# Two key chunks per step in the second layer, 12,000-byte key rows, and another order of the work on TensorE

## The reference, cut to what matters

```python
x = x + tanh(g_xattn[i]) * xattn(layernorm(x), ctx, ctx, ...)
x = x + tanh(g_ffn[i]) * ffn(layernorm(x), ...)

# layer 0, differential attention: 32 heads of 4 dims for q and k
a1 = softmax(q1 @ k1.T * SCALE) @ v ; a2 = softmax(q2 @ k2.T * SCALE) @ v
attn = a1 - lam * a2                       # then rms norm, subln_w, output projection

# layer 1, masked attention: 16 heads of 8 dims
scores = where(mask, finfo.min, (x @ Wq.T + bq) @ (ctx @ Wk.T + bk).T / sqrt(8))
out = softmax(scores) @ (ctx @ Wv.T + bv)  # then output projection
```

## Time and profile before

| | |
|---|---|
| median of 3 runs | 2350.72 us (2350.26 to 2360.24) |
| the profiled execution | 2361.65 us, its span on the core 2359.2 us |
| mean granted TensorE clock | 0.946 of full speed |
| main loop of layer 0 | from about 117 us to 1225 us |
| main loop of layer 1 | from about 1455 us to 2179 us |
| busy shares of the span | PE 93%, DVE 71%, ACT 64%, POOL 54% |

### The profile page before, as it was taken

One profiled execution on the slowest core, in us unless ns is written; L12 is line 12 of the kernel. 1 busy time (PEld: TensorE's weight loads), 2 busy tenths in 40 slices (PEclk: granted clock), 3 DMA queues, 4 the chain that ended last, 5 costly groups with the idle time before them and its releaser, 6 DMA issues. The chain is left out here.

```text
span 2359.2 us, 67435 instructions
## 1 busy us (share of the span) xinstructions
PE 2192.7 (93%) x27256; PEld 1303.0 (55%) x27256; DVE 1677.1 (71%) x3697; ACT 1507.8 (64%) x2133; POOL 1278.9 (54%) x1418
## 2 busy tenths in 40 slices
PE   4799999999999999999967957999999999999798
PEld 3255555555555555555536843666655666666576
DVE  3688888888888888888816555777766677774644
ACT  2177788777877778778763322767666667766322
POOL 5335655655654554655333445777766777762232
PEclk8599999999999999999997975999999999999699
DMA  3635344344444444444201027667665666661100
GB/s 105 128 77 113 96 98 109 101 94 108 106 97 99 112 96 95 115 93 94 48 7 57 24 61 149 137 142 137 143 131 120 127 144 140 138 126 24 54 1 16
DMA packets 113421, 227.82 MB, mean 97 GB/s; under 512 B 46052, under 2 KB 58596, under 8 KB 112612
## 3 DMA queue, kind: packets, MB, share of 16 engines
q1 hardware_dynamic: 113124, 223.67, 42.8%
HBM read 146.77 MB, written 76.48 MB: 95 GB/s over the span
## 5 line engine op out<-in xcount | busy, mean ns | idle before, releaser
L1061 ACT ACTIVATE probs<-score_ps 125x896 f32<-125x896 f32 x1152 | 1014.3, 915 | 210.3 <-PE score_ps L954 207.9
L1119 DVE TENSOR_REDUCE max_part<-max_ps 112x1 f32<-112x500 f32 x1024 | 654.7, 668 | 115.3 <-PE spare_ps L923 68.3
L970 PE MATMUL acc_ps<-probs,vext 125*32 125x224 f32 (+1 forms) x12288 | 673.2, 316 | 6.6 <-issue 6.1
L923 PE MATMUL max_ps<-kstack,qstack 48*112 48x500 f16 x1535 | 508.1, 405 | 4.9 <-DVE max_part L1119 2.6
L954 PE MATMUL score_ps<-qstack,kstack 50*125 50x224 f16 (+1 forms) x6144 | 454.8, 244 | 17.2 <-ACT probs L1061 13.9
L954 PEld LDWEIGHTS score_ps<-qstack,kstack 50*125 50x125 f16 x6144 | 344.4, 134 | 183.8 <-issue 122.2
L1116 DVE CUSTOM_DVE_ANT_0 kstack<-max_ps,kstack 112x500 f32<-112x500 f32 x511 | 335.3, 675 | 134.2 <-PE max_ps L923 80.1
L1119 DVE TENSOR_REDUCE max_part<-spare_ps 112x1 f32<-112x500 f32 x512 | 343.3, 670 | 64.6 <-PE max_ps L923 63.5
L970 PEld LDWEIGHTS acc_ps<-probs,vext 125*32 125x32 f32 x12288 | 261.7, 109 | 225.8 <-issue 156.5
L923 PE MATMUL spare_ps<-kstack,qstack 48*112 48x500 f16 x769 | 310.7, 404 | 20.2 <-issue 16.9
L923 PEld LDWEIGHTS max_ps<-kstack,qstack 48*112 48x112 f16 x1535 | 173.5, 129 | 143.4 <-issue 77.7
(11 more groups left out here) (200 smaller groups left out, 2697.8 us busy)
## 6 DMA issues: line engine op xcount, KB each, us to landing
kstack<-k_parts SPq DMA_DIRECT2D x384, 187.5 KB, 6.6
k_parts<-khl SPq DMA_DIRECT2D x128, 375.0 KB, 2.8
ctx_f<-in_ctx SPq DMA_DIRECT2D x32, 750.0 KB
ctx_f<-context_parts SPq DMA_DIRECT2D x32, 750.0 KB, 4.4
context_parts<-ctx_f SPq DMA_DIRECT2D x16, 750.0 KB, 3.8
context_parts<-kstack SPq DMA_DIRECT2D x16, 750.0 KB, 3.5
mask_in<-in_mask SPq DMA_DIRECT2D x128, 82.0 KB
qrows<-q_parts SPq DMA_DIRECT2D x384, 7.0 KB, 7.0
```

Source lines behind the costliest of these rows:

```text
L923: nc.tensor.matmul(room(("P", n, p))[0:PIECE, 0:TK], qstack[n % SLOTS][rows, c, PIECE * i:PIECE * (i + 1)], kstack[n % SLOTS][rows, c, TK ...
L970: last = nc.tensor.matmul(acc_ps[32 * j:32 * j + 32, TT * S * i:TT * S * (i + 1)].rearrange("p (s c) -> p s c", s=S), vext[n % SLOTS][:, t ...
L1061: nc.scalar.activation(probs[t % 2][:, 896 * h:896 * h + 896].rearrange("k (b c) -> k b c", b=2), score_ps[(t * H + h) % 2][0:KT, :, 0:448 ...
L1119: nc.vector.reduce_max(best, scores, AX.X).then_inc(s_red, 1)
```

## The change

1. **Layer 1 steps over two chunks.** `steps` is 6 instead of 12 there. A step has two scores (one per chunk), two pairs of search pieces, one `weigh` that covers both chunks (16 matmuls), and its preparations are merged into steps 1 to 5 (`where`): F and V0, then V1 and V2, then M and K0, then K1 and K2, then A. They go into the two banks of the score half that the first exponential has read, no longer into the search rooms. F is one job of four transposes and one drain in place of two. `AHEAD` is 3 steps (12 pieces) instead of 5 (10 pieces).
2. **The order of a step.** `weigh` is one call everywhere. `order_of` chooses one of four written orders by whether this step and the one before have a preparation other than A or M. Layer 0: `scores 0, pair 0, weigh, scores 1, pair 1, prepare`, except t = 1, where both scores stand first. Layer 1: steps 0 and 1 have both scores first; steps 2 to 4 run `scores 0, weigh, scores 1, pair 0, prepare, pair 1`; step 5 runs `scores 0, pair 0, scores 1, weigh, pair 1, prepare`.
3. **Key rows.** The columns of Wk are permuted at setup (`key_order`), so that the four `PAIRS` rows of a partition lie side by side in DRAM. A fill DMA reads 16 rows of 12,000 bytes instead of 64 of 3,000. The layer-1 key bias is loaded once more in that order, by eight DMAs of ScalarE's queue.
4. **Queues in layer 1.** POOL makes the additive mask before the score mask; SP loads the next mask only after both are made, and issues the next context load after `fill_m`.

```diff
+        self.uses_f = self.halves
+        self.steps = NKT if self.halves == 2 else NKT // 2
...
+        key_bias = [(columns[HALF * r + c:HALF * (r + 1):PAIRS, 2:4],
+                     a["columns"][HALF * r + HALF // PAIRS * c:HALF * r + HALF // PAIRS * (c + 1), :]) for r in range(2) for c in range(PAIRS)]
...
-                        link(nc.vector.tensor_copy(high, weight))
-                        link(nc.vector.tensor_tensor(low, weight, high, ALU.subtract))
+                        for part in [(weight, high, low)] if w else key_order(i, weight, high, low):
+                            link(nc.vector.tensor_copy(part[1], part[0]))
+                            link(nc.vector.tensor_tensor(part[2], part[0], part[1], ALU.subtract))
...
-        where = {("V", 0): (0, 2), ("F", 0): (1, 2), ("V", 1): (2, 2), ("F", 1): (3, 2), ("V", 2): (4, 2), ("K", 0): (5, 2),
-                 ("K", 1): (6, 2), ("M", 0): (7, 2), ("K", 2): (8, 2), ("A", 0): (10, 2)}
+        where = {("F", 0): (1, 1), ("V", 0): (1, 0), ("V", 1): (2, 0), ("V", 2): (2, 1), ("M", 0): (3, 1), ("K", 0): (3, 0),
+                 ("K", 1): (4, 0), ("K", 2): (4, 1), ("A", 0): (5, 1)}
...
+    AHEAD = 3 if L.masked else 5
...
+    ORDERS = {"both scores first": ("scores 0", "scores 1", "pair 0", "weigh", "pair 1", "prepare"),
+              "scores apart by a pair": ("scores 0", "pair 0", "scores 1", "weigh", "pair 1", "prepare"),
+              "scores apart by the product": ("scores 0", "pair 0", "weigh", "scores 1", "pair 1", "prepare"),
+              "pairs apart by preparation": ("scores 0", "weigh", "scores 1", "pair 0", "prepare", "pair 1")}
...
+        busy = [any(kind not in "AM" for kind, _, _ in at_step(*place)) for place in ((n, t), (n, t - 1) if t else (n - 1, STEPS - 1))]
+        if not busy[1]:
+            return ORDERS["both scores first"]
+        if L.masked and not busy[0]:
+            return ORDERS["scores apart by a pair"]
+        return ORDERS["pairs apart by preparation" if L.masked and busy[0] else "scores apart by the product" if busy[0] else "scores apart by the product"]
...
-                                         .rearrange("b (c d) k -> (b d) c k", c=PAIRS)).then_inc(s_ks[n % SLOTS], 16)
+                                         .rearrange("b (d c) k -> (b d) c k", c=PAIRS)).then_inc(s_ks[n % SLOTS], 16)
...
             def next_mask(n):
                 if L.masked:
                     sp.wait_ge(s_add, n)
+                    sp.wait_ge(s_big, n)
...
+                chunks = [(t, 0)] if H == 2 else [(2 * t + h, 896 * h) for h in range(2)]
+                for chunk, column in chunks:
+                    for i in range(2):
+                        for j in range(4):
+                            u = 4 * i + j
...
+                    for work in order_of(n, t):
+                        if work in ("scores 0", "scores 1"):
+                            scores(n, t, int(work[-1]))
+                        elif work in ("pair 0", "pair 1"):
+                            search(searched(n, t, int(work[-1])))
+                        elif work == "weigh" and weighed[0] >= 0:
+                            weigh(*weighed)
+                        elif work == "prepare":
+                            for user in at_step(n, t):
+                                use(user)
```

More of the change, by code:

```diff
@@ L490, in attend @@
     layer = 0 if L is L0 else 1
-    GD, GC, H = L.group_dims, L.group_cols, L.halves
+    GD, GC, H, STEPS = L.group_dims, L.group_cols, L.halves, L.steps
     K_WORDS = PAIRS * SK
@@ L575, in attend, with at_step @@
     LEAD = {"T": 3, "K": 3, "V": 2, "M": 1, "F": -1, "A": -1}
-    def at_step(n, t, side):
-        return [(kind, n + LEAD[kind], i) for (kind, i), place in where.items()
-                if place == (t, side) and 0 <= n + LEAD[kind] < B]
+    def at_step(n, t):
+        return [(kind, n + LEAD[kind], i) for (kind, i), (step, _) in where.items()
+                if step == t and 0 <= n + LEAD[kind] < B]
     def searched(n, t, k):
-        if 2 * k >= per_step:
-            return []
-        d, place = (1, early + t * per_step) if t < NKT - AHEAD else (2, (t - NKT + AHEAD) * per_step)
+        d, place = (1, early + t * per_step) if t < STEPS - AHEAD else (2, (t - STEPS + AHEAD) * per_step)
         return [("P", n + d, place + 2 * k + r) for r in range(2)] if n + d < B else []
@@ L592, in attend @@
     for n in range(B):
-        for t in range(NKT):
-            middle, last = at_step(n, t, 1), at_step(n, t, 2)
-            spare_uses += middle + last
-            if H == 2:
-                in_scores.update({user: n * NKT + t for user in middle})
-                middle = []
-            order += searched(n, t, 0) + middle + searched(n, t, 1) + last
+        for t in range(STEPS):
+            spare_uses += at_step(n, t)
+            in_scores.update({user: n * STEPS + t for user in at_step(n, t)})
+            order += searched(n, t, 0) + searched(n, t, 1)
     order += [(kind, B - 1, i) for kind, i in turnaround]
@@ L949, in scores @@
                                          big_eye[HALF * r:HALF * r + SQ, :], start=True, stop=False, skip_group_check=True)
-                here = PAIRS // H
-                for k in range(here):
+                for k, c in enumerate(columns):
                     for r in range(2):
                         rows = slice(HALF * r, HALF * r + KROWS + 2)
-                        last = nc.tensor.matmul(buf[0:KT, r, GC * k:GC * (k + 1)], kstack[n % SLOTS][rows, h * here + k, keys],
-                                                qstack[n % SLOTS][rows, h * here + k, :], start=not L.masked, stop=True,
+                        last = nc.tensor.matmul(buf[0:KT, r, GC * k:GC * (k + 1)], kstack[n % SLOTS][rows, c, keys],
+                                                qstack[n % SLOTS][rows, c, :], start=not L.masked, stop=True,
@@ L1150, in _ @@
             for n in range(B):
-                for t in range(NKT):
+                for t in range(STEPS):
                     for user in searched(n, t, 0):
                         reduce_piece(user)
-                    for user in at_step(n, t, 1):
-                        drain(user)
-                    if t == where["F", 1][0] + 1 and n:
+                    if t == where["F", L.uses_f - 1][0] + 1 and n:
                         reciprocals(n)
```

144 lines of the change are left out of this document (66 added, 78 removed).

## The result

The changed kernel takes **2362.72 us** (median of 19 runs, 2356.59 to 2369.72), the kernel before 2351.64 us beside it (19 runs, 2347.52 to 2366.03): a ratio of 1.0044, 95% interval 1.0032 to 1.0055. It is slower by 11 us. The forecast was 2298 us, with a range of 2264 to 2338: 65 us too low, and its sign was wrong.

What follows compares the result with a forecast made beforehand. PE, never idle in either main loop, was taken as the bound, so its work order sets the time. Layer 0 -27, layer 1 -29, setup +2.5, ends +1.5 sum to -52 from 2350.72: about 2298 us, range 2264 to 2338.

Steps and rivals of the forecast that it cites:

- Layer 0, "-27 us": Layer 0's new step order: elements of 34.0 to 34.1 us instead of 35.0, some 28 elements at 0.95, -27 us.
- The context load later: covered by PE, 0: Layer 1's later context load on SP's queue: hidden behind PE's work, costing 0 us.
- The loop is 15 + 1 + 5.5 = 21.5 us ... I take 21.25: Layer 1's key loop (K2 to keys, POOL's extra, PE's leg) sets the element: 21.25 us, 1.05 saved on 28, -29 us.
- +1: Layer 1's key loop: K2 closely follows K1, so POOL's low and high parts add 1 us (estimate 0.6 to 1.1).
- PE's own 20.85 us: Layer 1: PE's six steps, summed with their waits, take 20.85 us per element.
- M +0.5: Layer 1, t = 4: second scores wait for VectorE to drain M, adding 0.5 us.
- The fill: Key fill: 16 partitions per DMA are the likelier limit than row length; long rows bring only 0 to 3 us.
- Setup +2.5: Setup: four more small VectorE instructions and eight DMAs on ScalarE's queue cost 0 to +6 us, taken as +2.5.
- The loops eat it: Rival, chance 0.2: layer 0's exponential loop and layer 1's keys (21.8 or later) take the gain; 2315 to 2340 us.
- Gaps in PE's own stream: Rival, chance 0.07, slower: long-row fills issued fast starve PE in layer 1; 13 more gaps of 5.4 us give 2368.

Runs made afterwards that it cites:

- e4: Layer 0 of the changed kernel with layer 1 of the kernel before, the eight small bias loads of the setup kept: 2330.52 us.
- e3: Changed kernel with SP issuing layer 1's next context load where it stood before the change, ahead of the max rows' fill: 2341.53 us.
- e12: Kernel before with one part of the change: layer 1's next context load behind the max rows' fill, just before the key store: 2373.79 us.
- e1: Changed kernel with layer 1's key thirds projected at t = 2, 2 and 3, and keys stored ahead of the next context load: 2333.01 us.
- e9: e5 with VectorE draining M before the reductions of t = 3's second pair: 2279.49 us.
- e2: Changed kernel with layer 1's key rows of 3,000 bytes again instead of 12,000: 2370.48 us.
- e11: e9 with layer 1 key rows of 3,000 bytes and without the eight bias loads of the setup: 2281.93 us.
- e7: e1 with layer 1 key rows of 3,000 bytes instead of 12,000: 2340.10 us.
- e10: e5 with only SP's order changed, the next context loaded behind the key store, just before the fill: 2332.68 us.
- e5: Changed kernel with layer 1's values prepared at t = 0, 0, 1, keys at t = 2, 2, 3, and the context load back in its earlier place: 2310.37 us.
- e8: e1 with SP waiting before the second and third pair of layer 1's fill DMAs until the pair before has landed: 2466.37 us.

## Why the prediction was wrong

By its own steps:

- **Layer 0, "-27 us": right in mechanism, a little high.** 34.1 us an element, steps of 2.86 us where the exponential loop binds (first scores of the changed kernel at 711.89, 714.75 and 717.61), one wait of 0.80 at t = 1. The main loop gave 22.5 us: 0.9 and not 0.95 an element, and the last elements, which are bound by ScalarE, gave 1.8 back. e4 confirms it by itself.
- **"The context load later: covered by PE, 0": failed.** It cost 21 us (changed against e3), and 19 us in the kernel before (e12). The move was costed on PE alone; what counts is the DMA engines and SP's queue, where a 750 KB load now stood ahead of the store on which the loop hangs.
- **"The loop is 15 + 1 + 5.5 = 21.5 us ... I take 21.25": failed, the term that decided.** Without the context load's part e3 shows 22.54. Its turn above: PE's leg 5.7 where I had 5.5, and 5.95 in the mean, since half clock behind a wait makes it longer, which the sum left out; the low part 3.66 behind K2 (2.60 before; the "+1" was right); to the fill 1.75, mean 1.95, where one element of before gave 1.49, near the shortest of that kernel (mean 1.76); the fill 11.5, mean 11.3, where I had taken 10.9 from the end of a busy window of the DMA engines, which isn't the landing: that is 11.3 in the mean in the kernel before too. A loop of latencies is worth its means: at 22.54, above the old 22.3, layer 1 gains nothing. Then 21.25 was taken below my own sum, on the hope of the rows. (22.54 - 21.25) x 29 = 37 us.
- **PE's own 20.85 us: right within 0.2.** e1's elements without any stop take 21.05, with M's wait in them. e9's 20.90 is another order, with VectorE's wait in place of M's. "M +0.5": right, 0.57, though the profile names ScalarE.
- **The fill: right** that the rows are worth little (e2). That the 16 partitions are the limit instead is not tested by any run.
- **Setup +2.5: not shown.** The first A transpose of layer 0 comes 2.6 us later (190.95 against 188.33). But the first scores start only 1.1 us later (118.56 against 117.47), and the granted clock from 118 to 188 us was 0.88 against 0.93. Among the profiled executions with the eight loads the first scores start between 117.4 and 119.3, and in e11, without them, at 118.5. e4's sum used 2.6; without it it would be 2329, within its range as well, so e4 doesn't show the setup's part either.
- **Rivals.** "The loops eat it" named the mechanism (keys at 21.8 or later) and stopped at 2340, since it let layer 1 still gain 14 us. "Gaps in PE's own stream" ended at 2368, the nearest number, but the changed kernel has two small gaps; it came true only when the keys were freed (e1). What speaks against its form is that long rows aren't needed (e7). Its guess that PE is starved of something was right: of its instructions (e1).

The 65 us in sum: 21 for the context load, 37 for the rest of the loop, 4.5 for layer 0: 62, and 2 are left. Gaps nearly cancel in this: they and the half clock put e3's mean element 0.56 us above its median, and that of the kernel before 0.66.

## What to carry to other kernels

When an edit makes the bounding engine faster, write down the loop that closes through DMA with its mean legs over many turns, and compare it with the old period, not with the new sum: if it is longer than the old period, the edit is worth nothing until work at its head is moved earlier. Moving the key and value projections by one or two steps, one load on SP and one drain on VectorE, with no instruction fewer, took the changed kernel from 2362.7 to 2279.5 us. And an issue that moves on a queue is an edit of its own: look at what its bytes now stand in front of.

## What the runs showed of the hardware that I had not expected

- A 750 KB load issued 0.5 us ahead of a 750 KB store brings the store's landing from 2.8 to 6.2 us, and what follows it from 1.76 to 5.45 us behind the last input (e12).
- PE can run out of instructions. Its stops for nothing that the trace shows come once it hardly waits otherwise: 14 in 27 elements (e1), up to 4.13 us, with the clock at 0.7 behind one of them. All 90 in the traces stand at the same place of a block of 256 records, 1.2 to 2.0 us behind the landing of a 16 KB instruction packet. They are longer where context load and fill stand in the DMA engines as one block (e10), and e5's six were gone with another order on VectorE (e9).
- Six fill DMAs of 187.5 KB to 16 partitions each land within 11.3 us together in the mean; of three pairs, each issued behind the last one's landing, the second and third take 4.9 us each (e8).
